# A four-block transformer stack on one core: the router's work re-ordered around the shared expert

## The chip, the core and the metric

The kernel runs on one core of one Trainium2 chip. Five engines work side by side, each through its own list of instructions in order: TensorE (PE in the profile), VectorE (DVE), ScalarE (ACT), GpSimd (POOL) and SyncE (SP, which only starts transfers here). They meet only through semaphores. The metric is the time of one execution on the device in microseconds (us); lower is better.

## The reference

`x` holds 8 blocks of 128 rows with 256 columns, `ctx` the same. Four layers follow each other, each on the layer norm of `x` and added to it:

```python
x = x + L0_xattn(layernorm(x), ctx)      # 16 heads over 256 positions, rotary, batch of 8
x = x + L0_ffn(layernorm(x))             # mixture of experts: 2 of 16, and a shared expert
x = x + L1_xattn(layernorm(x), ctx)      # 32 heads of 8, q and k RMS-normalised
x = x + L1_ffn(layernorm(x))             # dense + low-rank experts, 2 of 16
```

The change is in the second layer. With `t` one of the 1024 rows of the normalised input:

```python
scores = sigmoid(t @ router.T)                       # 16 numbers per row
pick the 2 best of 4 groups by (scores + e_bias), then the 2 best experts in them
weights = scores[picked] / (sum + 1e-20)
routed = sum over picked e: weight_e * relu(t @ up_e)**2 @ down_e
shared = relu(t @ shared_up)**2 @ shared_down        # 512 inner columns
```

The layer norm is `(x - mean) / sqrt(var + 1e-5)`. The RMS norm of the third layer is `v * rsqrt(mean(v*v) + 1e-6)` over 8 numbers.

## The kernel before, in words

**Stages.** A: the first attention, a loop over the 8 blocks (`NB`), in each 8 steps (`PAIRS`); at a step PE makes scores (L662), ACT takes the exponential (L1112), PE multiplies by the values (`pv`, L677). B: the router and the shared expert, then the routed experts. C: the second attention in 8 slots of 4 steps. D: the last layer. Each engine's order is written out by hand, in Python loops over numbered half-steps ("spots"); nothing is scheduled by a tool.

**End of stage A.** For block 7 the normalisation of finished blocks is put into the attention's gaps on DVE: at spot 2 `norm_stats(0, 6)` (means, variances and reciprocal roots of blocks 0 to 5) and two `normalize_ffn`, which write the normalised rows to `ffn_x(b)`; at spot 6 `flip_back(6)`, a transpose that gives `o3`; at spot 9 the rest for blocks up to 6. PE's output product of block 6 (L685, at spot 9) waits for `flip_back(6)`. After the loop `flip(7)`, a division on POOL and `flip_back(7)` follow.

**Stage B on PE** is the list `B_USES`: the 7 turns of rows on TensorE (`xT`, L754), the output product of block 7 (`wm`), then pieces of the shared expert and of the router between each other. The shared expert has 8 pieces `n` (2 halves of the rows, 4 groups of 128 inner columns); `up` is L766, `activate` on ACT is a relu and a square (L1181, L1183), `down` is L775. The logits are made transposed for 512 rows at a time (`lgT`, L823), copied by DVE, and turned back by PE (`lg`, L833). DVE copies every turned block from PSUM to `xnT` (L1647), which `up` and the logits read. ACT's exponential (L1189) starts the choice of experts on DVE (L1659 to L1681), which ends in `hot16`. `rank` on PE (L802 to L807) counts with `hot16` how many rows stand ahead, and DVE makes `slots` of it (L1685 to L1698).

**After `slots`.** POOL sends the 1024 rows to the two experts' places with 16 indirect transfers (`sorted_x`, L1414); then SP loads them back in tiles of 256 rows, and a loop over 16 tile pairs turns (L912), multiplies (L924), activates and multiplies again (L936). Beside the scatter, PE, ACT and DVE prepare the keys of stage C: `project_keys` (L953), squares on ACT (L1196), sums and a reciprocal root over 128x256 (L1771, `rsqrt`), scaling (L1775), the weights of the experts (L1709 to L1716) and `rest_keys(0)` (L1782). All this stands ahead of the first tile in DVE's list.

**`rsqrt`** (L1445) is a bit-trick guess and three Newton steps; each instruction waits for the one before by a semaphore (`Steps`). It is used by every `norm_stats`, once for the keys and once for each of the 8 blocks of stage C.

PSUM has 8 banks; `misc(u)` gives a use its bank in turn, and two semaphores, `misc_full` and `misc_free`, count the uses.

## Time and profile before

| | us |
|---|---|
| median of 3 runs (lowest, highest) | 421.08 (418.58, 422.0) |
| the profiled execution | 418.32 |
| its span, first to last instruction | 416.6 |
| PE busy | 301.3 (72%) |
| DVE busy | 302.5 (73%) |
| ACT busy | 162.3 (39%) |
| POOL busy | 99.5 (24%) |

So 1.7 us of the profiled execution lie outside its span, and it is 2.8 us under the median. The mean granted TensorE clock is 0.865 of full speed (full is 2.4 GHz, the other level 1.2 GHz). In the strip of 40 slices of 10.4 us each, the router and the shared expert take slices 16 to 20:

```profile
PE   4257788878867666999926999133787897587795
PEld 3222444434433323366815998011454554353453
DVE  6977888988988687364483655186689888776894
ACT  1103557656655650233322776001544445160101
POOL 1234445535522201000771111464000000000000
PEclk9755999999999988999975999755788869695999
```

Each digit is the busy share of a slice in tenths. No engine is busy all the time, and which one is waited for changes from stage to stage; so the time is read from the chain of work that ended last, and from each engine's list where that chain passes.

### The profile page before, as it was taken

The page shows a single profiled execution, that of the slowest core. Times are in us where ns is not written, and L with a number is a line of the kernel's source. Part 1 is how long each engine was busy: PE and PEld are TensorE (multiplying, and loading weights), DVE is VectorE, ACT ScalarE, POOL GpSimd, SP SyncE. Part 2 cuts the span into 40 slices and gives each one's busy share as a digit, 9 for nine tenths or more (in the row PEclk, how much of TensorE's full clock was granted, in tenths as well). Part 3 has the DMA queues.
Part 4 walks back from the last instruction along what each step waited for, and adds up shares of the span by engine and source line. Part 5 has one row for each costly group of instructions (what it writes and reads, how often), then busy time and mean ns, then how long its engine had stood idle before and what let it go on. Part 6 is the DMA issues. An engine that isn't in the chain of part 4 may idle for free.

```text
span 416.6 us, 7271 instructions
## 1 busy us (share of the span) xinstructions
PE 301.3 (72%) x2634; PEld 184.9 (44%) x2634; DVE 302.5 (73%) x826; ACT 162.3 (39%) x252; POOL 99.5 (24%) x194
## 2 busy tenths in 40 slices
PE   4257788878867666999926999133787897587795
PEld 3222444434433323366815998011454554353453
DVE  6977888988988687364483655186689888776894
ACT  1103557656655650233322776001544445160101
POOL 1234445535522201000771111464000000000000
PEclk9755999999999988999975999755788869695999
DMA  7593466876787340000225666734365555400011
GB/s 238 154 264 108 119 211 170 235 242 148 223 251 220 121 162 0 0 2 0 99 98 183 203 212 198 222 101 133 119 192 179 179 176 179 140 2 1 2 50 50
DMA packets 76387, 58.19 MB, mean 140 GB/s; under 512 B 5056, under 2 KB 73152, under 8 KB 76352
## 3 DMA queue, kind: packets, MB, share of 16 engines
q1 hardware_dynamic: 66688, 42.68, 34.2%
q10 hardware_dynamic: 8128, 10.85, 8.2%
q0 software_dynamic: 1536, 4.20, 3.2%
q8 instruction: 21, 0.34, 0.3%
q14 instruction: 14, 0.11, 0.1%
HBM read 32.87 MB, written 24.64 MB: 138 GB/s over the span
## 4 chain that ended last, share of the span: by engine, by line
DVE 36%; PE 36%; issue 9%; DMA 8%; POOL 7%; ACT 1%; SPq 1%; POOLq 0%; DVEq 0%
DVE mx L1498 8%; PE psum L924 4%; POOL sorted_x L1414 4%; PE psum L936 3%; PE psum L766 3%; PE psum L626 3%; PE psum L775 2%; PE psum L677 2%; PE psum L754 2%; PE psum L912 2%; DVE stats L1465 2%; PE psum L641 2%; DVE pvT L1811 2%; DVE rope_ab L1487 2%; DVE rs_a L1454 2%
## 5 line engine op out<-in xcount | busy, mean ns | idle before, releaser
L1498 DVE TENSOR_REDUCE mx<-psum 128x2 f32<-128x512 f32 x128 | 81.0, 682 | 13.6 <-PE psum L641 12.5
L1112 ACT ACTIVATE prob<-psum 128x1024 f32<-128x1024 f32 x64 | 64.0, 1022 | 43.4 <-PE psum L662 43.3
L641 PE MATMUL psum<-kstk,qstk 64*128 64x256 bf16 x256 | 27.3, 295 | 21.4 <-DVE mx L1498 12.1
L1282 ACT ACTIVATE prob<-psum 128x1024 f32<-128x1024 f32 x32 | 32.6, 1024 | 23.1 <-PE psum L884 22.9
L677 PE MATMUL psum<-prob,vt 128*32 128x256 f32 x512 | 35.8, 391 | 5.8 <-ACT prob L1112 4.7
L444 POOL TENSOR_TENSOR parts<-qk_rest,parts 128x256 bf16<-128x256 f32 (+1 forms) x15 | 13.5, 902 | 68.4 <-ACT parts L1257 64.9
L662 PE MATMUL psum<-qstk,kstk 64*128 64x256 bf16 x256 | 25.2, 281 | 0.8 <-DMA qstk<-mT 0.8
L641 PEld LDWEIGHTS psum<-kstk,qstk 64*128 64x128 bf16 x256 | 9.8, 98 | 34.8 <-DVE mx L1498 23.9
L900 PE MATMUL psum<-prob,vt 128*32 128x128 f32 x512 | 23.9, 314 | 0.2 <-ACT prob L1282 0.2
L677 PEld LDWEIGHTS psum<-prob,vt 128*32 128x32 f32 x512 | 16.2, 110 | 14.2 <-ACT prob L1112 6.0
L754 PE MATMUL psum<-eye,xn 128*128 128x128 f32 x32 | 8.5, 355 | 19.3 <-DVE xn L1763 11.3
L1055 PE MATMUL psum<-wd,xnT 128*128 128x512 f32 x32 | 17.0, 682 | 2.8 <-DVE xall L1807 2.8
L1418 POOL DMA_INDIRECT wup<-sorted_y,slots x16 | 15.3, 955 | 15.5 <-DMA sorted_y<-qstk 11.0
L662 PEld LDWEIGHTS psum<-qstk,kstk 64*128 64x128 bf16 x256 | 8.5, 95 | 21.5 <-issue 12.5
L924 PE MATMUL psum<-xnT,qstk 128*128 128x128 f32 x124 | 17.8, 289 | 0.1
L863 PE MATMUL psum<-wc,xT 128*128 128x256 f32 x32 | 14.2, 591 | 4.8 <-DVE qk_rest L1801 4.2
L900 PEld LDWEIGHTS psum<-prob,vt 128*32 128x32 f32 x512 | 14.0, 122 | 7.4 <-issue 4.9
L1414 POOL DMA_INDIRECT sorted_x<-qstk,slots x8 | 7.9, 993 | 37.7 <-DVE slots L1698 35.5
L924 PEld LDWEIGHTS psum<-xnT,qstk 128*128 128x128 f32 x124 | 16.3, 203 | 0.9 <-issue 0.5
L1119 ACT CAST parts<-qk 128x512 bf16<-128x512 f32 x8 | 4.9, 618 | 29.5 <-POOL qk L438 17.1
L936 PE MATMUL psum<-wdn,act 128*128 x62 | 16.1, 381 | 0.0
L1181 ACT ACTIVATE rel<-psum 128x512 f32<-128x512 f32 x8 | 4.8, 597 | 28.8 <-PE psum L766 28.8
(238 smaller groups left out, 634.3 us busy)
## 6 DMA issues: line engine op xcount, KB each, us to landing
qstk<-stack_scratch SPq DMA_DIRECT2D x32, 256.0 KB, 3.9
kstk<-stack_scratch SPq DMA_DIRECT2D x30, 256.0 KB, 3.5
stack_scratch<-parts SPq DMA_DIRECT2D x23, 192.0 KB, 2.2
prob<-sorted_x SPq DMA_DIRECT2D x15, 256.0 KB, 3.1
stack_scratch<-parts SPq DMA_DIRECT2D x25, 128.0 KB, 2.2
sorted_x<-zero_row ACTq DMA_DIRECT2D x3, 1024.0 KB, 4.9
wup<-in_wup ACTq DMA_DIRECT2D x4, 640.0 KB, 4.7
wdn<-in_wdn ACTq DMA_DIRECT2D x4, 640.0 KB, 6.1
```

The lines of the kernel that those rows point to most:

```text
L641: last = nc.tensor.matmul(banks[s][:, nb * D:(nb + 1) * D], qstk[par][rows, pair, nb * P:(nb + 1) * P], kstk[par][rows, pair, :], start=Tr ...
L662: last = nc.tensor.matmul(exp_buf(k)[:, s, mb * D:(mb + 1) * D], kstk[b % SETS][rows, k, mb * P:(mb + 1) * P], qstk[b % SETS][rows, k, :], ...
L677: last = nc.tensor.matmul(pv_bank(1)[32 * j:32 * j + 32, g * D:(g + 1) * D], vt[b % 2][:, mb, 4 * t + j, 8:40] if low else vt[b % 2][:, mb ...
L754: last = nc.tensor.transpose(bank[:, n * P:(n + 1) * P], blk, eye[:])
L900: last = nc.tensor.matmul(pv_bank(k // 2)[32 * j:32 * j + 32, g * P:(g + 1) * P], v[:, 8 * k + h, 8:40], prob[k % 2][:, at * P:(at + 1) * ...
L924: last = nc.tensor.matmul(psum[:, n % 2, t_ * P:(t_ + 1) * P], tile_w(n, t_)[:, f * P:(f + 1) * P], tile_xT(n)[:, (2 * t_ + f) * P:(2 * t_ ...
L936: last = nc.tensor.matmul(psum[:, 2 + n % 2, t_ * D:(t_ + 1) * D], act2[n % 2][:, t_ * P:(t_ + 1) * P], w, start=True, stop=True)
L1055: last = nc.tensor.matmul(psum[:, b % 4, :], xnT[:, f, b * P:(b + 1) * P], wd[:, f, :], start=(f == 0), stop=(f == 1))
L1112: nc.scalar.activation(prob[(b * PAIRS + k) % 3][:], exp_buf(k).rearrange("p a n -> p (a n)"), ACT.Exp, scale=SCALE).then_inc(exp_done, 1)
L1282: nc.scalar.activation(prob[k % 2][:], exp_buf(k).rearrange("p a n -> p (a n)"), ACT.Exp, scale=SCALE).then_inc(exp_done, 1)
L1414: nc.gpsimd.indirect_dma_start(sorted_x, row_of(k, b), ffn_x(b), None).then_inc(scattered, 16)
L1498: nc.vector.tensor_reduce(mx[:, half, :, 4 * s + p4:4 * s + p4 + 1], bank.rearrange("n (b m) -> n b m", b=2), AX_X, ALU.max).then_inc(misc ...
```

## The change

1. **Roots.** `rsqrt` makes its first guess in two instructions instead of three (a multiplication by -0.5 takes the place of the shift and the -1.0), and takes two steps of four instructions (a third-order step, with its constants folded into gains) instead of three steps of three. Ten instructions in place of twelve, wherever it is called.
2. **Rows only centred.** `ffn_x(b)` holds `x - mean`; the root is not needed for it. The logits are multiplied by `rstd`, the shared expert's result and the experts' weights by `inv_var = rstd * rstd` (relu squared of a scaled row is its square times that). `add_shared` becomes `scalar_tensor_tensor` with that scalar.
3. **DVE at block 7.** Only `bn_stats` of blocks 0 to 3 stands ahead of `flip_back(6)`; means and centring follow it, and one `roots_ffn(0, 7)` stands behind all centring, ahead of `flip(7)`.
4. **Turned rows** are copied to `xnT` by ACT (`take_x`) instead of DVE; PE turns blocks 0 and 1 within the attention of block 7 (spots 12 and 14).
5. **Logits** are made per block, with the rows as the stationary operand (`logits`, 4 instructions a block, 16 columns each), in one bank; `lgT`, its copies and its turning back are gone.
6. **PE's order**: all turns, logits 0 to 3, the output product of block 7, logits 4 to 6, one `up`, the turn and logits of block 7, another `up`, four pairs of `down` and `up`, then `rank`, then the rest of the shared expert. New semaphores replace `misc_full` and `misc_free` there.

The core of the diff (moved but unchanged lines are left out):

```diff
@@ PE
+            def turn_x(b):
+                pe.wait_ge(xn_ready, NB + b + 1)
+                if b < 2:
+                    pe.wait_ge(misc_free, A_END)
+                else:
+                    pe.wait_ge(xt_free, b - 1)
+                for f in range(2):
+                    last = nc.tensor.transpose(xt_bank(b)[:, f * P:(f + 1) * P], ffn_x(b)[:, f * P:(f + 1) * P], eye[:])
+                last.then_inc(xt_full, 1)
...
+                    if b == NB - 1 and spot in (12, 14):
+                        turn_x(spot // 2 - 6)
...
+            def logits(b):
+
+                pe.wait_ge(xt_free, b + 1)
+                if b == 0:
+                    pe.wait_ge(pv_free, NB + 2)
+                for f in range(2):
+                    last = nc.tensor.matmul(lg_bank[:, b * NE:(b + 1) * NE], xnT[:, f, b * P:(b + 1) * P], wr[:, f, :],
+                                            start=(f == 0), stop=(f == 1))
+                last.then_inc(lg_full, 1)
...
+            for b in range(2, NB - 1):
+                turn_x(b)
+            for b in range(4):
+                logits(b)
+            pe.wait_ge(o3_ready, NB)
+            output(wm_bank).then_inc(wm_full, 1)
+            for b in range(4, NB - 1):
+                logits(b)
+            up(0, 0)
+            turn_x(NB - 1)
+            logits(NB - 1)
+            up(0, 1)
+            for n in range(4):
+                down(n // N_SHARED, n % N_SHARED)
+                up((n + 2) // N_SHARED, (n + 2) % N_SHARED)
+            rank()
+            for n in range(4, 2 * N_SHARED):
+                down(n // N_SHARED, n % N_SHARED)
+                if n + 2 < 2 * N_SHARED:
+                    up((n + 2) // N_SHARED, (n + 2) % N_SHARED)
@@ ACT
+            def take_x(b):
+                act.wait_ge(xt_full, b + 1)
+                nc.scalar.copy(xnT[:, :, b * P:(b + 1) * P], xt_bank(b)[:, 0:D].rearrange("p (f n) -> p f n", f=2)
+                               ).then_inc(xt_free, 1)
+
+            for b in range(NB):
+                take_x(b)
+            activate(0, 0)
+            act.wait_ge(lg_taken, 1)
+            nc.scalar.activation(sc[:], sc[:], ACT.Exp, scale=-1.0).then_inc(sig_ready, 1)
+            for n in range(1, 2 * N_SHARED):
+                activate(n // N_SHARED, n % N_SHARED)
@@ DVE
-                for _ in range(3):
+                for gain in (1.0, STEP_GAIN):
                     steps.then(nc.vector.tensor_tensor(a, o, v, ALU.mult))
-                    steps.then(nc.vector.scalar_tensor_tensor(out=a, in0=a, scalar=-0.5, in1=o,
-                                                              op0=ALU.mult, op1=ALU.mult))
-                    steps.then(nc.vector.scalar_tensor_tensor(out=o, in0=a, scalar=1.5, in1=o,
+                    steps.then(nc.vector.tensor_tensor(a, a, o, ALU.mult))
+                    steps.then(nc.vector.scalar_tensor_tensor(out=a, in0=a, scalar=-10 / 3 * gain, in1=a,
+                                                              op0=ALU.add, op1=ALU.mult))
+                    steps.then(nc.vector.scalar_tensor_tensor(out=o, in0=a, scalar=5.0 * gain ** 2, in1=o,
                                                               op0=ALU.add, op1=ALU.mult))
...
                     if spot == 2 and b == NB - 1:
-                        norm_stats(0, B_EARLY)
+                        bn_stats_of(0, 4)
+                    if spot == 6 and b == NB - 1:
+                        steps.then(bn_stats_of(4, B_EARLY - 4))
+                        means(0, B_EARLY)
...
-                        norm_stats(B_EARLY, 1)
-                        normalize_ffn(B_EARLY)
+                        steps.then(bn_stats_of(B_EARLY, 1))
+                        means(B_EARLY, 1)
+                        for early in range(2, NB - 1):
+                            center_ffn(early)
+                        roots_ffn(0, NB - 1)
...
+            dve.wait_ge(lg_full, NB)
+            nc.vector.tensor_tensor(sc[:], lg_bank.rearrange("p (b e) -> p b e", e=NE), spread(rstd[:], NB, NE), ALU.mult
+                                    ).then_inc(lg_taken, 1)
+            nc.vector.tensor_tensor(inv_var[:], rstd[:], rstd[:], ALU.mult)
```

The three places where instructions move are shown as lists, in program order. First DVE around the transpose `o<-o` of block 6 (`flip_back(6)`; `rs_v`, `rs_a`, `rstd` are the root's numbers, `qstk` and `kstk` hold `ffn_x`). Before:

```order
L1465 BN_STATS stats<-xall 128x6 x6
L1472 BN_AGGR mv<-stats 128x2 x6
L1448 TENSOR_SCALAR rs_v<-mv 128x6
L1449 TENSOR_SCALAR rs_a<-rs_v 128x6
L1451 TENSOR_SCALAR rstd<-rs_a 128x6
...
L1481 TENSOR_SCALAR qstk<-xall,mv,rstd 128x256 x2
L1521 STREAM_TRANSPOSE o<-o 128x256
L1506 SCALAR_TENSOR_TENSOR xall<-psum,cb,xall 128x256
```

and DVE at the same place after the change:

```order
L1487 BN_STATS stats<-xall 128x6 x4
L1550 STREAM_TRANSPOSE o<-o 128x256
L1487 BN_STATS stats<-xall 128x6 x2
L1504 BN_AGGR mv<-stats 128x2 x6
L1508 TENSOR_SCALAR qstk<-xall,mv 128x256 x2
L1535 SCALAR_TENSOR_TENSOR xall<-psum,cb,xall 128x256
L1487 BN_STATS stats<-xall 128x6
L1504 BN_AGGR mv<-stats 128x2
L1508 TENSOR_SCALAR qstk<-xall,mv 128x256 x2
L1508 TENSOR_SCALAR kstk<-xall,mv 128x256 x3
L1469 TENSOR_SCALAR rs_v<-mv 128x7
```

Two statistics, six means, twelve instructions of roots and two normalisations stood ahead of the transpose and now stand behind it; the roots come once, behind the centring.

Second, PE from the last two products with the values (`psum<-prob,vt`) to `rank` (`psum<-hot,before`). Before, up to the second half's logits (L766 is `up`, L775 `down`, L754 a turn):

```order
L677 MATMUL psum<-prob,vt 32x256 x8
L754 MATMUL psum<-eye,qstk 128x128 x8
L754 MATMUL psum<-eye,kstk 128x128 x6
L685 MATMUL psum<-o,wa 128x256
L766 MATMUL psum<-xnT,wup 128x512 x4
L775 MATMUL psum<-wdn,act 128x256 x4
L823 MATMUL psum<-xnT,wr 16x512 x2
L754 MATMUL psum<-eye,kstk 128x128 x2
L823 MATMUL psum<-xnT,wr 16x512 x2
```

and PE after the change (L791 is `up`, L802 `down`, L705 a turn, L815 the logits):

```order
L705 MATMUL psum<-eye,qstk 128x128 x4
L690 MATMUL psum<-prob,vt 32x256 x8
L705 MATMUL psum<-eye,qstk 128x128 x4
L705 MATMUL psum<-eye,kstk 128x128 x6
L815 MATMUL psum<-wr,xnT 128x16 x8
L709 MATMUL psum<-o,wa 128x256
L815 MATMUL psum<-wr,xnT 128x16 x6
L791 MATMUL psum<-xnT,wup 128x512 x2
L705 MATMUL psum<-eye,kstk 128x128 x2
L815 MATMUL psum<-wr,xnT 128x16 x2
L791 MATMUL psum<-xnT,wup 128x512 x2
L802 MATMUL psum<-wdn,act 128x256 x4
```

Behind these, seven `up` and six `down` stood ahead of `rank` in all; now six `up` and four `down` do, and four `down` and two `up` follow it (before two and one).

## Rows read from the trace of the kernel before

**Rows 1.** The chain that ended last, in order of time: start, us, what
```profile
190.55 1.72 PE psum L766 x4
192.26 1.73 PE psum L775 x8
...
194.26 0.21 PE psum L807 x8
...
196.38 0.19 DVE slots L1698
...
219.49 2.90 DMA prob<-sorted_x
...
224.47 2.01 PE psum L924 x8
```

**Rows 2.** Timeline of PE: start, us, engine, line, names, count [idle before <-releaser]
```profile
139.25 0.60 PE L685 MATMUL psum<-o,wa 128*128 128x256 f32 x2
...
152.46 1.19 PE L685 MATMUL psum<-o,wa 128*128 128x256 f32 x2 [1.98 <-DVE o L1521]
...
157.46 1.07 PE L677 MATMUL psum<-prob,vt 128*32 128x256 f32 x16 [1.12 <-ACT prob L1112]
...
162.52 1.79 PE L754 MATMUL psum<-eye,kstk 128*128 128x128 f32 x6 [0.19 <-DVE xnT L1647]
...
172.65 0.44 PE L754 MATMUL psum<-eye,kstk 128*128 128x128 f32 x2
...
216.31 1.12 PE L964 MATMUL psum<-eye,qkn 128*128 128x128 f32 x4 [7.34 <-DVE qkn L1775]
...
372.40 1.07 PE L851 MATMUL psum<-w,eh 128*128 128x16 f32 x8 [0.96 <-DVE eh L1874]
```

**Rows 3.** Timeline of DVE, end of stage A and choice of experts
```profile
146.24 1.99 DVE L1465 BATCH_NORM_STATS2 stats<-xall 128x6 f32<-128x256 f32 x6
...
151.22 0.73 DVE L1481 TENSOR_SCALAR qstk<-xall,mv,rstd 128x256 f32<-128x256 f32 x2
...
158.69 0.71 DVE L1512 STREAM_TRANSPOSE pvT<-psum 128x512 f32<-128x512 f32 x1
...
160.67 0.45 DVE L1521 STREAM_TRANSPOSE o<-o 128x256 f32<-128x256 f32 x1 [0.88 <-POOL o L1365]
...
180.44 0.23 DVE L1659 TENSOR_SCALAR sc<-sc 128x128 f32<-128x128 f32 x1 [3.94 <-ACT sc L1189]
...
189.53 0.29 DVE L1681 TENSOR_TENSOR hot<-hot_all 128x128 bf16<-128x128 f32 x1
194.50 0.17 DVE L1685 TENSOR_SCALAR pages<-psum 128x16 int32<-128x16 f32 x1 [4.68 <-PE psum L807]
```

**Rows 4.** Timeline of ACT: a copy, and two exponentials of block 7
```profile
139.88 0.37 ACT L1130 COPY vt<-psum 128x256 f32<-128x256 f32 x1 [0.27 <-PE psum L685]
...
154.23 1.02 ACT L1112 ACTIVATE prob<-psum 128x1024 f32<-128x1024 f32 x1 [2.69 <-PE psum L662]
```

**Rows 5.** Windows of 2 us: PE, PEld, DVE, ACT, POOL busy, PEclk, DMA, GB/s
```profile
166.00:168.00 2.00, 2.00 (x6) 0.95 (x5) 1.69 (x10) 0.51 (x1) 0.00 (x0) 0.98 0.00 0
```

**Rows 6.** Timeline of DVE beside the scatter, the keys and the first tile
```profile
210.69 0.29 DVE L1449 TENSOR_SCALAR qk<-qk 128x256 int32<-128x256 int32 x1
...
219.71 0.69 DVE L1782 TENSOR_TENSOR qk_rest<-psum,kstk 128x512 f32<-128x512 f32 x1
223.65 0.69 DVE L1733 COPY xnT<-psum 128x512 f32<-128x512 f32 x1 [3.25 <-PE psum L912]
```

**Rows 7.** Timeline of DVE in stage C: a root over 128x32, first and last
```profile
306.69 0.24 DVE L1448 TENSOR_SCALAR rs_v<-ss,eps_v 128x32 f32<-128x32 f32 x1
...
309.42 0.42 DVE L1793 TENSOR_TENSOR qkn<-psum,rs 128x256 f32<-128x256 f32 x1
```

**Rows 8.** Timeline of POOL: two of the 16 scatters, the second beside DVE's wide root
```profile
202.75 0.96 POOL L1414 DMA_INDIRECT sorted_x<-qstk,slots  x1 [0.30 <-issue]
...
212.98 1.08 POOL L1414 DMA_INDIRECT sorted_x<-kstk,slots  x1 [0.30 <-issue]
```

254 lines of the change are left out of this document (107 added, 147 removed).

## The prediction

> **What bounds the kernel now.** I read the chain that ended last first. Between the end of the first attention and the first routed tile it runs: PE's pieces of the shared expert, `rank`, DVE to `slots`, 16 scatters on POOL, the load of the tiles, PE's tile loop [rows 1]. The reader is to see that ahead of `rank` stand an `up` of 1.72 us and a `down` of 1.73, and that no wait for DVE is named there. DVE's timeline says why: `hot16` was done at 189.53 + 0.29 = 189.82, and DVE then idled 4.68 us until `rank`'s result [rows 3]. So the router's result lay ready for over 4 us while PE worked through its list; what stands in PE's list ahead of `rank` is the bound, not the choice of experts. `rank` ended at 194.47 and `slots` at 196.57 [rows 1].
>
> Next, the end of the attention in PE's timeline: the output product of block 6 at 152.46 had waited 1.98 us for DVE's transpose, and ran 1.19 us instead of the 0.60 of its like at 139.25; the last product with the values ran from 157.46 to 158.53 [rows 2]. ACT's exponential at 154.23 had idled 2.69 us behind it [rows 4]. DVE made its roots and normalisations ahead of that transpose [rows 3].
>
> Last, what lies in the shadow of the scatter. From `slots` (196.57) to the tile loads' end (219.49 + 2.90 = 222.39) is 25.8 us [rows 1]. DVE meanwhile finished the keys at 219.71 + 0.69 = 220.40 and waited 3.25 us before the first tile's copy at 223.65 [rows 6]. That is the slack which anything made later on PE, ACT or DVE after `rank` can use.
>
> **The change, part by part** (clock times are those of the profiled execution).
>
> *End of the attention.* After the change the transpose of block 6 stands behind four statistics of 0.33 us (1.99 for six, from 146.24 [rows 3]), so it ends at about 148.0, before PE asks for it at 152.46 - 1.98 = 150.48 [rows 2]. The output product then runs 150.5 to 151.1 at 0.60; scores, the two exponentials of 1.02 [rows 4] and the products of 1.07 [rows 2] follow in turn: scores to 151.4, the exponential behind its predecessor 151.5 to 152.5, products to 152.6, scores to 153.0, the last exponential to 154.0, the last products 154.05 to 155.1. Gain 158.5 - 155.1 = **3.4 us**. If the clock falls all the same, the product costs 1.19 instead of 0.60, and with the others slow as well I count back 1.5 us: bounds 1.9 and 3.4. I take 3.4, because the idle time ahead of the slow spell is what is removed.
> DVE's moved work stays off PE's way: from 151.1 a sum, a statistic and a mean (about 1.1), five centrings at 0.33 (0.73 for two [rows 3], the second's tail overlapping), ten root instructions at about 0.225 (below) end at 156.1; then flip, reciprocal, POOL's division and the transpose back, 160.67 + 0.45 - 158.69 = 2.4 us from the flip's start [rows 3], so `o3` is there at 158.5. PE wants it at 159.8 (next sum).
>
> *PE's list from there to `rank`.* Before: 158.53 to 194.47, 35.9 us. After, if PE never waits:
> - 5 turns; ACT copies instead of DVE (0.37 against about 0.4 [rows 4]), two banks in turn; six rows (three turns) took 1.79 us [rows 2]: 5 x 0.55 = 2.75, bounds 2.2 and 3.0;
> - 32 logit instructions; nearest is L851, same shape 128x16, eight in 1.07 with the last one's tail: 32 x 0.125 = 4.0;
> - output product 0.60;
> - 6 `up` x 1.72 = 10.3 and 4 `down` x 1.73 = 6.9 [rows 1];
> - the eighth turn 0.44 [rows 2], its copy 0.37 and the handing over: 0.95; `rank` 0.5.
>
> Sum 26.0, so `rank` ends at 155.1 + 26.0 = 181.1, **9.9 us** gained beside the 3.4. Does PE wait? The eighth turn needs block 7 centred: output product at 160.4, sum, statistic, mean, centring on DVE 1.6 us more: 162.0; PE is in `up` until 163.6. `hot16`: the last logits end at 165.0, DVE scales them (0.3), ACT's exponential stands behind `activate(0, 0)` and ends at 166.1, and from there the choice takes 189.82 - 180.44 = 9.4 us [rows 3]: 175.5. PE reaches `rank` at 180.6, so 5 us of slack there. The same 2.1 us lead to `slots` at 183.2, against 196.57: **13.3 us** earlier.
>
> *After `rank`.* Now four `down` and two `up` (10.3 us) follow where two and one stood (5.2): relative to `rank`, PE's keys come 5.2 us later. DVE gets back 0.8 us in the wide root (one instruction like the shift, 0.29 alone and 0.33 in step [rows 6], one of about 0.46) and pays 0.2 for the multiplication by `inv_var`. `add_shared` in its new form costs at most 0.15 us more for each of 8, hidden, since DVE waits for the keys' squares behind it. So DVE is free for the first tile at 220.4 - 13.3 + 5.2 - 0.6 = 211.7, while the tile path would want it at 223.65 - 13.3 = 210.3: **1.3 us lost**. Against that stands TensorE's clock. Before, PE idled 7.34 us ahead of turning the keys at 216.31 [rows 2] and again until the tiles; the first tile's eight products took 2.01 us [rows 1], at 1.2 GHz, where eight at 2.4 GHz are about 0.9. After, keys and tiles follow each other without a gap, from 207.4 on, and PE, steadily at work from 162.52, had a granted clock of 0.98 (2.4 GHz nearly throughout) from 166 on [rows 2, 5]. If so, the first products and turns gain up to 1.7 us. I take the two together as +0.4 gained; bounds -1.3 and +1.7.
>
> *Roots elsewhere.* A root over 128x32 took 309.42 - 306.69 = 2.73 us for 12 instructions, 0.227 each [rows 7]; two less save 0.45. On the chain lie: the first layer norm ahead of the first loads, seven of the eight roots of stage C (the third one, of block 2, runs while PE waits for a transfer), the two of stage D. 10 x 0.43 = **4.3 us**; bounds 2 (stage C partly waits for PE) and 5.
>
> **Sum.** 3.4 + 9.9 + 0.4 + 4.3 = 18.0 us off 418.32 gives 400.3. The median of the runs was 2.8 us above the profiled execution; on its scale the sum is 403.1. I forecast between them: **402 us**. Its own range, from the bounds (1.5 and 1.7 and 2.3 us less gained, not all at once; 1.3 and 0.7 more): 397 to 406.
>
> **Rivals.**
> *The keys become the bound (0.18).* For it: 5.2 us of delay against 3.25 of slack, and ACT, PE and DVE hand over to each other there four times, with PE at half clock if it idles. If PE's clock is down for the six remaining pieces and the keys as well, or down in the turns and logits (where PE hands every block to ACT), 4 to 7 us of the gain go: 406 to 410. Against: pieces of the shared expert follow without gap.
> *The gain is larger (0.07).* PE wins back clock through the denser stages: below 397.
> *It does not do what it says (0.04).* `slots` come earlier but the tile loop starts as before, since something in the shadow (the keys) takes it all: only the roots and the attention's end remain, or the roots alone: 414 to 421.
> *Slower (0.03).* One mechanism: POOL's scatters. Each takes 0.96 us; those beside DVE's wide root took 1.08, so DVE's work cost them 0.12 [rows 8]. PE and DVE now have more work beside them. The gain is eaten at 18.0 / 16 = 1.1 us more for each, that is when one takes 2.1 us; at 2.4 us (1.44 more, 16 times, 23 us) the end is 425. Against: nearly the same DVE instructions ran beside them before, and nothing stretched by more than 0.12.
> The Trainium skill (SBUF — State Buffer, "SBUF: two separate sides") says that GpSimd cannot write the descriptors of its own transfers while VectorE runs in a two-port mode; the page counts float32 copies within SBUF among the causes, and `tensor_tensor` and `tensor_reduce` not. By that rule the new work should hold up no scatter, since the root is now nearly all of two-operand forms; the 0.12 us were lost beside such forms too, which the rule does not give. Neither changes the sum.
>
> **How the numbers follow.** The forecast (397 to 406) gets 0.68, the rivals 0.18, 0.07, 0.04 and 0.03. Half the keys' case and the larger gain are taken in: 396 to 409 holds over 8 in 10. A measurement of this kernel can tell about 1% from no change. Faster by over 1% are the first three cases: 0.93; within 1%: 0.04; slower: 0.03.
>
> **What would show it.** Right: no idle time on PE ahead of the output product of block 6; last products with the values at about 155; `rank` near 180.6, no wait named for DVE's `hot16`, DVE idle some 5 us ahead of it; `slots` near 183; first tile's copy at 211 to 212 with hardly an idle time ahead; 10 instructions a root. Wrong: PE idle between turns and ACT's copies of more than 0.2 us each; logits of more than 0.15 us an instruction; a granted clock of 0.5 between 155 and 165 or at the first tile; POOL's transfers above 1.1 us; stage C as long as before.

## The result

The changed kernel took 408.71 us (median of 4 runs, 407.19 to 410.48) where the kernel before took 421.54 (4 runs, 418.58 to 422.55): a ratio of 0.971, with a 95% interval of 0.964 to 0.978. Forecast were 402.0 us, with 397 to 406 as its own range and 396 to 409 as the wider one: the sign was right, and the time lies outside the first range and at the very end of the second. Run again unaltered on other chips, the same kernel took 409.74, 422.51 and 419.95 us, with before at 421.48, 420.99 and 419.82 beside it. So there are two things to explain: 6.7 us that were missing at once, and 10 us more that are lost on some chips. Ratios and intervals, here and below, leave out disturbed executions, over 1.5% above the fastest of their kernel, so a ratio need not be the quotient of two medians (of "old root" below two of four executions are left, of "flip behind" two of eight). The profiled execution took 407.19 us, with a span of 405.4 against 416.6 before.

The page of the changed kernel, first part and granted clock (columns as on the page of before):

```profile
span 405.4 us, 7267 instructions
PE 300.0 (74%) x2650; PEld 187.4 (46%) x2650; DVE 290.6 (72%) x777; ACT 164.4 (41%) x260; POOL 98.9 (24%) x194
PEclk9755799999999998899979999555998989777997
```

PE's timeline from the last block's attention to the last logits (start, us, engine, line, names, count, idle before):

```profile
150.69 0.70 PE L709 MATMUL psum<-o,wa 128*128 128x256 f32 x2
...
154.39 1.07 PE L690 MATMUL psum<-prob,vt 128*32 128x256 f32 x16 [0.53 <-ACT prob L1129]
...
157.59 2.14 PE L815 MATMUL psum<-wr,xnT 128*128 128x16 f32 x16
159.57 1.20 PE L709 MATMUL psum<-o,wa 128*128 128x256 f32 x2
160.56 2.58 PE L815 MATMUL psum<-wr,xnT 128*128 128x16 f32 x12
162.98 3.37 PE L791 MATMUL psum<-xnT,wup 128*128 128x512 f32 x4
```

Two things are to be seen against [rows 2]. The output product of block 6 at 150.69 waits for nothing, and the last products with the values end at 154.39 + 1.07 = 155.46 instead of 158.53. But from 159.57 on every piece takes nearly twice what it should: the output product 1.20, the twelve logits 2.58 (0.215 each), an `up` 3.37. The windows of 2 us (PE, PEld, DVE, ACT, POOL busy, PEclk, DMA, GB/s) say why:

```profile
158.00:160.00 2.00, 2.00 (x14) 2.00 (x15) 0.37 (x1) 0.16 (x1) 0.98 (x3) 0.75 0.00 0
160.00:162.00 2.00, 2.00 (x10) 1.82 (x9) 1.04 (x3) 0.00 (x0) 0.00 (x0) 0.50 0.03 8
162.00:164.00 2.00, 2.00 (x8) 1.48 (x8) 1.69 (x11) 0.00 (x0) 0.00 (x0) 0.50 0.00 0
164.00:166.00 2.00, 2.00 (x4) 0.87 (x3) 0.20 (x2) 0.00 (x0) 0.00 (x0) 0.54 0.00 0
166.00:168.00 2.00, 1.54 (x8) 0.89 (x7) 0.24 (x2) 1.36 (x3) 0.00 (x0) 1.00 0.00 0
```

PE is busy in all of it but the last window, and yet has 1.2 GHz (0.50) for six microseconds. DVE's timeline at the rank and at the first tile:

```profile
183.75 0.17 DVE L1713 TENSOR_SCALAR pages<-psum 128x16 int32<-128x16 f32 x1 [5.94 <-PE psum L828]
...
185.63 0.17 DVE L1726 CAST slots<-slot_f 128x16 int32<-128x16 f32 x1
...
213.50 0.69 DVE L1813 TENSOR_TENSOR qk_rest<-psum,kstk 128x512 f32<-128x512 f32 x1
214.11 1.28 DVE L1763 COPY xnT<-psum 128x512 f32<-128x512 f32 x2
```

The rank came at 183.7, and DVE had waited 5.94 us for it, so PE's list is still what bounds the slots. At the first tile DVE had no idle time left: where it waited 3.25 us before [rows 6], the keys now bound it.

Stage by stage, all in us and all from the two profiled executions:

| stretch | before | after | gain | forecast |
|---|---|---|---|---|
| start to the last block's maxima in TensorE's hands | 143.99 | 144.27 | -0.3 | +0.4 |
| to the last product with the values | 14.54 | 11.19 | 3.35 | 3.4 |
| to the rank's end | 35.9 | 28.25 | 7.7 | 9.9 |
| rank to the end of the tile loop | 66.5 | 66.4 | 0.1 | 0.4 |
| tile loop to the first expert sum | 9.8 | 9.15 | 0.65 | 0 |
| stage C, to the last norm's statistics | 82.7 | 81.8 | 0.9 | 3.0 |
| stage D and the end | 63.1 | 64.3 | -1.2 | +0.9 |

This table is one profile against one, and some of its rows don't repeat. The changed kernel was profiled four times in all, and the kernel before twice:

| stretch | before | before again | changed | again | third | fourth |
|---|---|---|---|---|---|---|
| last block's maxima to the last product with the values | 14.5 | 14.5 | 11.2 | 14.4 | 14.4 | 14.5 |
| from there to the rank's end | 35.9 | 36.0 | 28.25 | 31.3 | 31.3 | 28.3 |
| stage C | 82.7 | 83.6 | 81.8 | 83.9 | 82.9 | 82.4 |
| stage D and the end | 63.1 | 62.2 | 64.3 | 63.1 | 60.5 | 64.3 |

So the 3.35 us at the end of the attention were there in one profile of four, and the slots, at 185.6 us in the first, came at 190.5 to 191.0 in the other three. PE's timeline of the third profile there, and two windows, show why (columns as above):

```profile
149.64 1.93 PE L690 MATMUL psum<-prob,vt 128*32 128x256 f32 x16 [0.69 <-ACT prob L1129]
...
152.04 1.22 PE L709 MATMUL psum<-o,wa 128*128 128x256 f32 x2
```
```profile
144.00:146.00 2.00, 1.36 (x12) 0.44 (x8) 1.49 (x4) 1.03 (x2) 0.34 (x1) 0.50 0.31 65
...
150.00:152.00 2.00, 2.00 (x20) 0.53 (x12) 0.00 (x0) 0.50 (x1) 0.00 (x0) 0.50 0.26 62
```

The output product of block 6 waits for nothing here either, but PE has 1.2 GHz from 144 to 154 and makes each set of products with the values in 1.93 us instead of 1.07. Of the 16 profiles of the changed kernel and its variants, 11 have this spell and 14.4 to 14.5 us in the stretch, and 5 have 11.2. What decides between the two stays open.

In stage C the chain of the first profile after the change runs through SyncE and its transfers, where that of the first profile before hardly did. The chain that ended last, part of block 3 (start, us, what):

```profile
282.31 3.80 DMA stack_scratch<-parts
286.12 0.36 SPq L589
...
288.10 3.39 DMA stack_scratch<-wa
...
291.55 2.27 DMA kstk<-stack_scratch
```

and the wait that goes with it (engine, line, waited for: us in total, times, longest):

```profile
PE psum L901 <- DMA qstk<-stack_scratch: 7.0, 4, 2.6
```

### The profile page after: what moved, and what is told of

It reads as the page before. It is cut to its first block, busy times and chain, and to the rows that moved or that the text cites. A ratio compares the mean times of both kernels' runs of the same rounds, so it can differ in the third digit from the quotient of the medians.

```text
span 405.4 us, 7267 instructions
## 1 busy us (share of the span) xinstructions
PE 300.0 (74%) x2650; PEld 187.4 (46%) x2650; DVE 290.6 (72%) x777; ACT 164.4 (41%) x260; POOL 98.9 (24%) x194
## 4 chain that ended last, share of the span: by engine, by line
PE 41%; DVE 30%; DMA 12%; issue 6%; POOL 4%; SPq 4%; ACT 3%; DVEq 0%; POOLq 0%
DVE mx L1527 8%; PE psum L791 4%; DMA stack_scratch<-parts 4%; PE psum L941 4%; PE psum L690 4%; PE psum L802 3%; PE psum L953 3%; PE psum L639 3%; PE psum L654 2%; PE psum L1088 2%; DVE rope_ab L1516 2%; PE psum L970 2%; PE psum L780 2%; DMA stack_scratch<-wa 2%; DMA kstk<-stack_scratch 2%
## 5 line engine op out<-in xcount | busy, mean ns | idle before, releaser
L1527 DVE TENSOR_REDUCE mx<-psum 128x2 f32<-128x512 f32 x128 | 81.1, 682 | 15.7 <-PE psum L654 14.4
L1303 ACT ACTIVATE prob<-psum 128x1024 f32<-128x1024 f32 x32 | 32.5, 1023 | 26.9 <-PE psum L901 26.7
L690 PE MATMUL psum<-prob,vt 128*32 128x256 f32 x512 | 35.9, 392 | 5.3 <-ACT prob L1129 4.2
L917 PE MATMUL psum<-prob,vt 128*32 128x128 f32 x512 | 22.6, 301 | 0.2 <-ACT prob L1303 0.2
L901 PE MATMUL psum<-qstk,kstk 64*128 64x128 bf16 x256 | 13.9, 236 | 7.3 <-DMA qstk<-stack_scratch 7.0
L675 PEld LDWEIGHTS psum<-qstk,kstk 64*128 64x128 bf16 x256 | 8.5, 95 | 20.7 <-issue 13.3
L941 PE MATMUL psum<-xnT,qstk 128*128 128x128 f32 x124 | 16.8, 278 | 1.3 <-DVE xnT L1763 1.2
L917 PEld LDWEIGHTS psum<-prob,vt 128*32 128x32 f32 x512 | 13.3, 117 | 7.3 <-issue 4.3
L791 PE MATMUL psum<-xnT,wup 128*128 128x512 f32 x32 | 16.6, 646 | 0.0
L941 PEld LDWEIGHTS psum<-xnT,qstk 128*128 128x128 f32 x124 | 15.2, 192 | 2.3 <-DVE xnT L1763 1.6
```

Source lines behind the costliest of these rows:

```text
L675: last = nc.tensor.matmul(exp_buf(k)[:, s, mb * D:(mb + 1) * D], kstk[b % SETS][rows, k, mb * P:(mb + 1) * P], qstk[b % SETS][rows, k, :], ...
L690: last = nc.tensor.matmul(pv_bank(1)[32 * j:32 * j + 32, g * D:(g + 1) * D], vt[b % 2][:, mb, 4 * t + j, 8:40] if low else vt[b % 2][:, mb ...
L791: last = nc.tensor.matmul(psum[:, n % 2, :], wup[:, f, NE + g, :], xnT[:, f, c * HALF:(c + 1) * HALF], start=(f == 0), stop=(f == 1))
L917: last = nc.tensor.matmul(pv_bank(k // 2)[32 * j:32 * j + 32, g * P:(g + 1) * P], v[:, 8 * k + h, 8:40], prob[k % 2][:, at * P:(at + 1) * ...
L941: last = nc.tensor.matmul(psum[:, n % 2, t_ * P:(t_ + 1) * P], tile_w(n, t_)[:, f * P:(f + 1) * P], tile_xT(n)[:, (2 * t_ + f) * P:(2 * t_ ...
L1303: nc.scalar.activation(prob[k % 2][:], exp_buf(k).rearrange("p a n -> p (a n)"), ACT.Exp, scale=SCALE).then_inc(exp_done, 1)
```

## The experiments

Eighteen runs followed, in sets that each shared a chip and the runs of before; a ratio is to those of before in the same set. The last four columns are from the profiled execution: "attention's end" is the last block's maxima to the last product with the values, "values to slots" goes from there to the slots, "slots to tile" to the first tile's copy, and "stage C" is the first expert sum to the last norm's statistics.

| kernel | median, us | ratio (95%) | attention's end | values to slots | slots to tile | stage C |
|---|---|---|---|---|---|---|
| before | 421.5 | | 14.5 | 37.9 | 27.3 | 82.7 |
| changed | 408.7 | 0.971 (0.964 to 0.978) | 11.2 | 30.2 | 28.5 | 81.8 |
| set 1: changed, old root | 413.8 | | 14.5 | 30.2 | 29.2 | 84.1 |
| before, new root | 420.2 | 1.000 (0.996 to 1.003) | 14.4 | 39.6 | 27.0 | 82.3 |
| changed, queries first | 404.1 | 0.960 (0.957 to 0.964) | 14.5 | 30.2 | 28.5 | 77.7 |
| before, queries first | 420.2 | 0.999 (0.996 to 1.002) | 14.5 | 37.9 | 27.1 | 82.7 |
| set 2: weights late | 420.4 | 0.999 (0.995 to 1.003) | 14.4 | 33.2 | 37.6 | 82.3 |
| logits behind | 419.8 | 1.001 (0.998 to 1.004) | 14.5 | 26.9 | 38.8 | 81.8 |
| flip behind | 423.5 | 0.990 (0.983 to 0.997) | 14.5 | 30.2 | 38.9 | 82.9 |
| rank early | 420.4 | 1.000 (0.996 to 1.003) | 11.2 | 26.8 | 40.8 | 81.9 |
| set 3: changed again | 422.5 | 1.002 (0.996 to 1.008) | 14.4 | 33.2 | 38.9 | 83.9 |
| before again | 421.2 | 0.998 (0.990 to 1.007) | 14.5 | 37.9 | 28.7 | 83.6 |
| queries first, weights late | 417.2 | 0.985 (0.977 to 0.994) | 11.2 | 30.1 | 37.7 | 80.7 |
| turns twice | 418.4 | 0.989 (0.981 to 0.997) | 11.2 | 27.7 | 39.4 | 82.3 |
| set 4: changed, third time | 409.7 | 0.974 (0.966 to 0.981) | 14.4 | 33.2 | 28.5 | 82.9 |
| VectorE copies | 414.6 | 0.977 (0.968 to 0.986) | 11.2 | 30.2 | 31.1 | 84.2 |
| scatters behind | 428.8 | one run | 14.5 | 30.2 | 45.3 | 83.6 |
| VectorE copies, queries first | 409.6 | 0.970 (0.963 to 0.977) | 14.4 | 30.2 | 31.1 | 79.6 |
| set 5: changed, fourth time | 420.0 | 2 runs | 14.5 | 30.2 | 38.8 | 82.4 |
| VectorE copies, queries first | 418.9 | 0.997 (0.994 to 1.000) | 14.5 | 30.2 | 39.9 | 78.1 |

### Where the roots' gain went: SyncE's list

The roots were to give 3.0 us in stage C and gave 0.9. Two kernels change the root alone, in either kernel:

```
...
-                for gain in (1.0, STEP_GAIN):
+                for _ in range(3):
...
-                    steps.then(nc.vector.tensor_tensor(a, a, o, ALU.mult))
-                    steps.then(nc.vector.scalar_tensor_tensor(out=a, in0=a, scalar=-10 / 3 * gain, in1=a,
-                                                              op0=ALU.add, op1=ALU.mult))
+                    steps.then(nc.vector.scalar_tensor_tensor(out=a, in0=a, scalar=-0.5, in1=o,
+                                                              op0=ALU.mult, op1=ALU.mult))
...
```

(this is the changed kernel with the old root, whose first guess in three instructions comes back too; the other kernel has the same edit the other way round, in the kernel before)

> The changed kernel with the root of before (12 instructions). Prediction on record: the ten-step root is worth about 4.3 us outside the router, so this kernel would be 4 to 5 us slower than the changed one. Theory now (SyncE's list of transfers sets the pace of the second attention, so that shorter roots only make VectorE wait longer): the stretch from the first expert sum (259.3 us in the changed kernel) to the statistics of the last norm (341.2), 81.9 us there, stays within 1.2 us, and the whole is at most 2.5 us slower, of which the wide root of the keys is 0.8.

> The kernel before with the ten-step root alone. Prediction on record: 4.3 us and more faster (416.5 on the median's scale). Theory now: the stretch of the second attention was 82.8 us before and was close to SyncE's pace already, so it gains at most 1.5 us; all in all 1 to 2.5 us faster than before.

and two exchange a pair of transfers in SyncE's list of stage C, again in either kernel:

```
                 keys_c_to_dram(b)
+                queries_c_to_dram(b)
                 sp.wait_ge(st_full, NB * PAIRS + (b - 2) * C_STEPS + 4)
                 keys_c_from_dram(b)
-                queries_c_to_dram(b)
                 queries_c_from_dram(b)
```

> The changed kernel, and in the second attention SyncE writes the queries of a block ahead of loading its keys, so that it no longer stands still for the 3 us in which the keys' write lands. If SyncE's list sets the pace, the stretch of 81.9 us falls by 2 to 4 us and TensorE no longer waits for the query loads (7.0 us there in the changed kernel); if VectorE does, it stays within 0.7.

> The kernel before with the same exchange in SyncE's list. If SyncE's pace bound only the changed kernel (whose roots are shorter), the stretch of 82.8 us stays within 0.7 here; if it bound both, it falls by 1 to 2 us. Rival: the transfers themselves take longer when queries and keys are written together, and it grows.

Measured: the new root in before gives nothing (ratio 1.000; 1 to 2.5 us had been expected), and neither does the exchange in before (0.999). The old root in the changed kernel has 84.1 us in stage C, more than the 1.2 us above 81.8 that were expected; but the changed kernel itself had up to 83.9 in its four profiles, so this run alone doesn't show what the old root costs there. The exchange in the changed kernel takes stage C to 77.7 and the whole to 404.1 us, and PE's waits at L901 for `qstk<-stack_scratch` are gone from its waits. That chip had no run of the changed kernel, but sets 3 to 5 have one each: beside it on the same chip, kernels with the exchange have 80.7 against 83.9, 79.6 against 82.9 and 78.1 against 82.4.

PE's scores, which waited for no transfer in the first profile of before, do wait with the new root in it, and do in the second profile of before itself too (in this order; columns as above):

```profile
PE psum L886 <- DMA qstk<-stack_scratch: 6.3, 4, 2.1
```
```profile
PE psum L884 <- DMA qstk<-stack_scratch: 4.5, 3, 2.3
```

What follows: stage C has two limits close to each other, DVE's work for a block, and SyncE's list, where the queries' write stands behind the keys' load, which stands behind the landing of the keys' write. With the old root or the old order of transfers the stage takes 82 to 84 us, whichever of the two it is, and so close that either can come last from one profile to the next. Either edit alone is hidden by the other limit; with both it takes 77.7 us, 5 less than the kernel before with the exchange alone on the same chip, and 78.1 to 80.7 in the other sets.

### TensorE's clock ahead of the rank

PE's list took 28.25 us instead of 26.0, with PE at 1.2 GHz for about 7 us while it was busy. Three kernels move or add work there. In "logits behind" PE takes the output product, the first `up`, the last turn, and then all logits together; in "turns twice" the turns of blocks 2 to 7 run twice, into the same bank, to fill PE's idle time of the attention (the result stays the same); in "flip behind" DVE's order at block 7 is that of before, with the centrings and the root ahead of the flip. The first two edits:

```
-            for b in range(4):
-                logits(b)
             pe.wait_ge(o3_ready, NB)
             output(wm_bank).then_inc(wm_full, 1)
-            for b in range(4, NB - 1):
-                logits(b)
             up(0, 0)
             turn_x(NB - 1)
-            logits(NB - 1)
+            for b in range(NB):
+                logits(b)
             up(0, 1)
```
```
-                for f in range(2):
+                for f in (0, 1, 0, 1) if b >= 2 else (0, 1):
```

> The changed kernel with the output product of block 7 and one up ahead of all logits, which then stand in one piece behind the eighth turn. In the changed kernel the granted clock fell to 0.5 at 158.5 and came back at 166. If the logits' small products (16 columns) let the clock fall, the output product and the up run at 2.4 GHz and a fall comes later or not at all; if the spell was set by what came before 158 (turns with idle time between), it falls at the same place and costs the same 3.6 us. From the last product with the values (155.5) to rank's end (183.7) are 28.2 us in the changed kernel; 25 without a slow spell.

> The changed kernel with each turn of the blocks 2 to 7 done twice (16 us of TensorE's otherwise idle waits filled at most; no result is changed). Theory that TensorE's idle time ahead of 158 us costs the granted clock behind it: with more work there the clock falls less or later, and the stretch from the last value product to the rank (28.2 us) shrinks by up to 3.6 us, less the 0.35 us that the last block's second turn adds. Rival, that the fall comes from the work that is there anyway (full busyness): it stays 28.2 us or longer, with the same level of 0.5 in it.

> The changed kernel with VectorE's order at block 7 as before: statistics, means and roots of six blocks and two centrings ahead of the transpose of block 6. By the prediction TensorE waits again, about 1.5 to 2 us, at the output product of block 6, and the last product with the values ends 1.5 to 3.4 us later against the start of block 7. Rival: TensorE's gap was only moved, and the distance stays within 0.5.

PE's timeline of "logits behind" from the output product on:

```profile
162.76 0.70 PE L709 MATMUL psum<-o,wa 128*128 128x256 f32 x2 [0.33 <-DVE o L1547]
163.30 1.88 PE L791 MATMUL psum<-xnT,wup 128*128 128x512 f32 x4
...
165.46 3.64 PE L815 MATMUL psum<-wr,xnT 128*128 128x16 f32 x32
```

and the window in which only logits run (columns as above):

```profile
167.00:169.00 2.00, 2.00 (x20) 2.00 (x19) 0.00 (x0) 0.19 (x1) 0.00 (x0) 1.00 0.00 0
```

Here the 32 logits take 3.64 us. This profile has the earlier spell, 0.50 from 147 to 155, but from the last product with the values on the clock stays at 2.4 GHz, and PE's list from the last product with the values (160.14) to the rank (184.82 + 0.35) takes 25.0 us. So the forecast's sum for this list (26.0) was right for a full clock, even a little high, and the clock is what was missing: 28.25 - 25.0 = 3.2 us. "Turns twice" keeps the clock at 1.00 as well and takes 2.5 us off the stretch to the slots, though it does more work. The two differ in what they keep. "Turns twice" keeps the order, with 16 logits ahead of the output product, and fills the waits for ACT's copies; "logits behind" keeps those waits and puts an `up` ahead of the narrow products. Neither the waits alone nor the early logits alone made the clock fall in these profiles, both together did, in all 14 profiles of kernels that have both. Each of the two exceptions rests on one profile. How long the spell lasts isn't fixed: until 166 in the first profile, until 174 in the third of the same kernel, with 33.2 us to the slots instead of 30.2.

"Flip behind" puts roots and centrings ahead of the transpose of block 6 again, which the output product of that block waits for; what they cost is to be read in the attention's end. It took 14.5 us, and PE waited for no transpose: the transpose ended at 152.46, and PE, at 1.2 GHz by then, asked for it at 153.28 only. The changed kernel itself has 14.4 to 14.5 us whenever that spell comes. So in the spell this edit of the change is worth nothing; at full clock, where PE asked at 150.69, it wasn't measured. The stretch behind, to the slots, stays at 30.2 us.

### The keys, now the bound of the first tile

```
-            expert_weights()
             rest_keys(0)
...
                 if n in (4, 8, 11):
                     rest_keys(n // 4 + n // 11)
+                if n == 6:
+                    expert_weights()
```

> The changed kernel with the experts' weights (7 VectorE instructions, 1.9 us) moved from ahead of the first tile to behind the sixth. If VectorE's work on the keys is what the first tile now waits for, the time from slots (185.8) to the first copy of a tile (214.1), 28.3 us, falls by 1.3 to 1.9 us, down to the 26 to 27 us that scatter and load take. If the scatter and the load are the bound, it stays within 0.4.

In "rank early" one pair of `down` and `up` is moved from ahead of the rank to behind it:

```
-            for n in range(4):
+            for n in range(3):
...
-            for n in range(4, 2 * N_SHARED):
+            for n in range(3, 2 * N_SHARED):
```

> The changed kernel with rank one pair of down and up (3.45 us) earlier; the choice is ready by then (VectorE idled from 177.7 to 183.7). If TensorE's whole list and the keys behind it are the bound, slots come 3.4 us earlier and the first tile's copy and everything behind it do not move (within 0.5). If slots are the bound, the first tile's copy comes 2.5 to 3.4 us earlier.

Both fell on a chip where the whole stretch was longer (next part), and are compared with their neighbours there. Taking the weights' seven instructions from ahead of the first tile shortens the stretch by 1.2 us (37.6 against 38.8, and 37.7 against 38.9 in set 3), a little under the 1.3 to 1.9 that were expected. An earlier rank moves the slots 3.4 us forward and lengthens the stretch behind them by 2.0, so that the copy comes 1.4 us earlier, where at most 0.5 or at least 2.5 was expected; with late signals in that stretch it decides nothing. So the work on the keys bounds the first tile after the change, as forecast, by the first run and by the missing idle time in the first profile.

### The same kernel at 422 us: signals that come late beside the scatters

Sets 2, 3 and 5 gave medians of 417.2 to 423.5 us for everything built on the changed kernel. Is it the variants or the chip? The controls, unaltered:

> The changed kernel itself, unaltered. Four variants of it (the owner's weights later, the logits together behind, the flip behind, the rank earlier) took 420 to 423 us where the kernel before took 420; in all four profiles 10 us are lost at one place, between the slots and the first tile's copy (37.6 to 40.8 us, against 28.5 in the changed kernel's profile): ScalarE stands up to 5.8 us ahead of its copies of the context and its squares, while the scatters run. Two of the variants change only VectorE's order and cannot touch ScalarE's list. If the stall belongs to the chip or the hour and not to the variants, this kernel shows it in some runs too, and its time is near 420 when it does and 408 to 410 when it doesn't; if it belongs to the variants, this kernel stays at 407 to 411 with 28.5 us at that place.

> The kernel before, unaltered, for its profile on this chip. Its time stayed within 418 to 423 us on both chips, so a stall of ScalarE beside the scatters should be absent from it: slots to first copy 27.3 us, as in its first profile. If it has the stall as well, other stretches are shorter than in the first profile.

> The changed kernel with SyncE's queries ahead of its key loads (it gave 404.1 us alone) and the experts' weights computed at the seventh pair of tiles instead of ahead of the first. If the keys bound the first tile's copy, the second edit takes 1.3 to 1.9 us off the 28.5 us from the slots to that copy, and the whole comes to 402 to 403 us; if ScalarE's stall comes, 10 us are lost there instead and it comes to 412 to 415.

It is the chip, or the hour: the unaltered kernel took 422.5 us, and loses 10.4 us between the slots and the first tile. The kernel with queries first and the weights late took 417.2 us, more than the 412 to 415 that were expected with that loss. ACT's timeline there, in that control, and PE's:

```profile
204.18 0.60 ACT L1217 ACTIVATE sq<-psum 128x512 f32<-128x512 f32 x1 [2.97 <-PE psum L970]
207.02 0.59 ACT L1240 COPY ctx_all<-psum 128x512 f32<-128x512 f32 x1 [2.25 <-remote]
213.37 0.60 ACT L1217 ACTIVATE rel<-psum 128x512 f32<-128x512 f32 x1 [5.77 <-remote]
214.81 0.59 ACT L1240 COPY ctx_all<-psum 128x512 f32<-128x512 f32 x1 [0.84 <-remote]
```
```profile
202.53 0.60 PE L962 MATMUL psum<-eye,ctx_all 128*128 128x128 f32 x4
202.96 1.89 PE L970 MATMUL psum<-wc,ctx_all 128*128 128x256 f32 x8
...
207.75 2.60 PE L970 MATMUL psum<-wc,ctx_all 128*128 128x256 f32 x8 [2.46 <-issue]
```

The copy at 207.02 needs the turn that PE's row ends at 203.13; the square at 213.37 needs the product that ends at 204.85: it came 8.5 us late, with ACT idle for 5.77 of them. (The ends of PE's rows are modelled, so these profiles don't tell whether the result or only its signal was late; PE took ACT's signals within 0.2 us here.) In the first profile the four squares follow each other at 1.7 to 2.2 us with no such wait, though the scatters run beside them there too. "Remote" means that the profile knows no sender for what ended the wait. All of it lies beside the second half of POOL's 16 scatters, which themselves take their usual 0.96 us (POOL's timeline of the same run, the first, the ninth and the last):

```profile
192.04 1.20 POOL L1435 DMA_INDIRECT sorted_x<-qstk,slots  x1 [30.61 <-DVE slots L1726]
...
202.42 0.96 POOL L1435 DMA_INDIRECT sorted_x<-kstk,slots  x1 [0.30 <-issue]
...
211.27 0.96 POOL L1435 DMA_INDIRECT sorted_x<-kstk,slots  x1 [0.30 <-issue]
```

The kernel before meets it too, against what was expected, in its profile of the same set (ACT's timeline):

```profile
210.26 0.60 ACT L1196 ACTIVATE rel<-psum 128x512 f32<-128x512 f32 x1 [2.30 <-remote]
215.24 0.60 ACT L1196 ACTIVATE act<-psum 128x512 f32<-128x512 f32 x1 [4.38 <-remote]
```

These are 6.7 us of waits, but only 1.5 us more from the slots to the first tile. Before, the context's first copy came 3.8 us behind the slots, so that only the last two squares were left when the signals grew late, and the 3.25 us of slack at the first tile [rows 6] took most of that. The change brings the rank, and so the scatters, ahead of six pieces of the shared expert; the first copy now comes 9.0 us behind the slots, nearly the whole chain of copies and squares lies in the scatters' second half, and there is no slack behind it. "Rank early" goes one step further that way and has the longest stretch of all (40.8).

Is it ACT's own? The copies and squares go to VectorE (lines shortened):

```
-                nc.scalar.copy(ctx_all[...], psum[:, 4 + p % 2, :])
+                nc.vector.tensor_copy(ctx_all[...], psum[:, 4 + p % 2, :])
-                nc.scalar.activation(k_squares(p), psum[:, p, :], ACT.Square)
+                steps.then(nc.vector.tensor_copy(k_squares(p), psum[:, p, :]))
+                nc.vector.tensor_tensor(k_squares(p), k_squares(p), psum[:, p, :], ALU.mult)
```

and for the cause the scatters are held until the last square:

```
             pool.wait_ge(slots_ready, 1)
+            pool.wait_ge(k_squared, CTX_PAIRS)
```

> The changed kernel, unaltered, as the control of this set. It shows one of the two states seen so far: 407 to 411 us with 28.5 us from the slots to the first tile's copy, or 420 to 425 us with 38 to 40 us there and ScalarE standing about 9 us in all ahead of its copies and squares.

> The changed kernel with the copies of the turned context and the squares of the keys on VectorE instead of ScalarE (a square takes two instructions there, a copy and a product, so four times 0.6 us more). If the stall is ScalarE's own, the 38 to 40 us from the slots to the first tile's copy fall to 30 to 32 (28.5 plus the 2.4 us at most that VectorE's longer squares cost), and the time to about 411 to 414. If whatever engine does this work beside the scatters is held up, VectorE shows the same waits with its inputs ready and the stretch stays at 38 us or more. In the state without the stall this kernel is 1 to 3 us slower than the control.

> The changed kernel with GpSimd's 16 scatters held until the last square of the keys is done; only for what ScalarE does beside them. If the scatters hold ScalarE up, its copies and squares run as in the first profile (last square 17.8 us behind the slots), and the stall, if it lasts as long as the scatters, meets the next ScalarE instructions behind the gate. If they are not the cause, ScalarE stands 9 us as in the control, at the same place. The gathers of rows start some 17 us later than in the first profile in either case, so the time is 420 to 428 us and says nothing by itself.

> The kernel with VectorE's copies and squares, and SyncE's queries ahead of its key loads besides (alone it took 4.6 us off the changed kernel). In the state with the stall: 406 to 410 us, which would beat both kernels there by over 2%. In the state without it: 404 to 407, no better than the SyncE order alone (404.1).

This set fell on a chip that doesn't do it: the control took 409.7 us with 28.5 us in the stretch. So it says nothing on the cause; the run with the scatters held back shows no wait, but there was none to be taken away. It tells the price of VectorE's longer squares, 2.6 us (31.1 against 28.5). The last set:

> The changed kernel as the control once more: 407 to 411 us with 28.5 us from the slots to the first tile's copy, or 420 to 425 us with 38 to 40 us there.

> VectorE's copies and squares with SyncE's queries first, again. It took 409.6 us (31.1 us from the slots to the first tile's copy) on a chip without the stall. If the control shows the stall and it is ScalarE's own, this kernel keeps 31 us there and 406 to 412 us in all; if any engine is held up that does this work then, it shows 38 us or more there and 415 us or more.

Here the control has it (420.0 us, 38.8 in the stretch), and so has the kernel with VectorE's copies. DVE's timeline of that kernel, and PE's:

```profile
205.62 0.69 DVE L1849 COPY ctx_all<-psum 128x512 f32<-128x512 f32 x1 [4.18 <-remote]
...
213.37 0.69 DVE L1849 COPY ctx_all<-psum 128x512 f32<-128x512 f32 x1 [5.02 <-remote]
```
```profile
203.39 0.60 PE L962 MATMUL psum<-eye,ctx_all 128*128 128x128 f32 x4
```

The turn that ended at 203.99 reached DVE at 213.37. So it isn't ScalarE's own: the engine that takes PE's result waits, whichever it is, and moving the work from one to the other is no cure (39.9 us, and 418.9 in all). What holds the signal up stays open. It was seen only beside scatters, and in all nine profiles of the changed kernel and its variants that had it, the last late signal came 2.4 to 2.6 us after the end of the last scatter's row; that points at the scatters. But the one run that takes them away from that place was on a chip without it, so it isn't shown. Nor is it shown that the chip decides, and not the hour: the five sets ran on five chips, each once. And only one execution of each kernel was profiled; on the chips with late signals some others were as fast as 412.4 and 414.0 us, and what happened in them isn't known.

## Why the forecast was right, and where it was wrong

Two steps failed. The roots outside the router were put at 4.3 us on the chain and came to -0.6 in the three stretches where they lie, which is 4.9 of the 6.9 us missing between the two profiled executions. And TensorE's clock was taken as full from the end of the attention to the rank, which cost 2.2 there at once and, in the other profiles of the same kernel, most of the gain at the attention's end as well.

- **End of the attention, 3.4 us.** The first profile has 3.35, but by luck. The transpose of block 6 was ready and the output product ran without a wait, in all four profiles; but in three of them PE had 1.2 GHz all the same, and the gain was 0.1. The reason given for 3.4, that the idle time ahead of the slow spell is what is removed, is wrong: the spell comes without it. And the bound of 1.9 for that case is too high, since the spell was some 10 us long, where before it had been 3 to 4.
- **PE's list to the rank, 9.9 us.** The step that failed: it gave 7.7 in the first profile, and 4.6 in two others. Its sum was made at full clock throughout, and "logits behind" shows that it holds at full clock (25.0 us for 26.0). The changed kernel has 1.2 GHz from about 159 to 166, which cost 3.2 us against the 25.0. The forecast had named the sign of it (a granted clock of 0.5 between 155 and 165) among what would prove it wrong, and had a price for it in the keys' case, but put nothing of it in the sum, and PE was without idle time when the clock fell.
- **What hides the router.** Right: the choice of experts was ready 5.9 us ahead of the rank, as the forecast's 5. The lead on the slots was 196.57 - (185.63 + 0.17) = 10.8 instead of 13.3, which is mostly the clock again; in the other three profiles the slots stood at 190.7 to 191.2.
- **After the rank, +0.4.** Nearly right, by both of its terms: the keys bound the first tile (no idle time ahead of the copy), and the first tile's eight products took 1.16 us instead of 2.01. The sum came to +0.1.
- **Roots elsewhere, 4.3 us.** This step failed: -0.3 of 0.4 at the start, 0.9 of 3.0 in stage C, -1.2 of 0.9 in stage D. The root itself gave what was reckoned (ten instructions, 0.83 us less for the wide one). In stage C the step failed that counted seven roots on the chain because DVE was on it before: SyncE's list stood close behind it. The exchange in SyncE's list brings out the rest, and more. At the start the root's gain was there (the first row maxima begin at 22.20 instead of 23.23) and was gone by 144; PE's clock was 0.67 against 0.71 from 20 to 60. At the end the last products ran at 1.2 GHz (next row, PE's timeline of the changed kernel; before, the same four instructions took 1.13 us), which made the way from the last adapter's input to the end 2.8 us longer. The third profile of the same kernel has 2.4 GHz there and 60.5 us in stage D, so the program doesn't fix where such a spell falls; whether the change makes one likelier there isn't shown:

```profile
396.10 2.07 PE L1088 MATMUL psum<-wb,wxaT 128*128 128x256 f32 x4
```

- **The scale and the range.** The forecast stood 1.7 us above its own sum on the profiled scale (400.3), because the median of before was higher than its profile. The profile after was 1.5 us below its median too, so that was right. The lower end of its own range, 397, doesn't follow from its terms: 400.3 less 2.0 is 398.3.
- **The rival of the keys (0.18, 406 to 410)** gave the right time. Its mechanism, PE's clock down in the turns and logits, is what took 3.2 us; the keys' delay took no more than the 1.3 us that the forecast had in its sum, and the rest was lost in stages C and D, of which the rival said nothing.
- **The rival of the scatters (0.03, slower)** did not happen as it was told: a scatter took 0.96 or 0.97 us in the changed kernel (the first 1.21, as before), with no stretching at all, also beside `tensor_tensor` and reductions, which is what the Trainium skill's rule (SBUF — State Buffer, "SBUF: two separate sides") gives. Single scatters were stretched in two variants, to 1.11 us with the old root and to 1.18 where they were held back. But the place was right, as sets 2, 3 and 5 show: what is put beside the scatters can lose all that the change gains, by late signals and not by slower scatters.

## What to carry to other kernels

When work is made shorter on the chain, look for the second limit right behind it, an in-order transfer queue above all: here two edits that were each worth nothing on the kernel before took stage C down by 5 us together. Price a list of small products at half clock too, and put wide products ahead of the narrow ones; the same instructions took 28.2 us or more in one order and 25.0, in one profile, in another. Profile a kernel more than once before a stretch's gain is put down to an edit: 3.35 us at the attention's end were 0.1 in three other profiles. And measure on more than one chip before a gain is believed: the best version depends on it, with 404.1 us (0.960 of before) for the changed kernel with queries first where signals were prompt, and 417.2 us (0.985) for the same with the weights late where they weren't.

## What the runs showed of the hardware

- TensorE's granted clock fell to 1.2 GHz while the engine was fully busy, with turns, short waits and 16-column products ahead of the fall, and stayed there for some 7 us in one profile and 14 in another of the same kernel. Either filling the waits or a 512-column product ahead of the narrow ones kept it at 2.4 GHz, in one profile each.
- The same program met a slow spell in one execution and not in another: at the attention's end 1.2 GHz for some 10 us in 11 of 16 profiles, with no idle time of PE over 1.9 us ahead, and 2.4 GHz throughout in 5.
- On three of the chips a signal from TensorE reached ScalarE or VectorE up to 10 us after the row of the work had ended (the product that ended at 196.74 and the square at 206.70 in "turns twice"), in the second half of 16 scatters, with both kernels; in the profiles of the first result and of sets 1 and 4 never.
- A write to DRAM whose landing a queue waits for before its next transfer cost that queue 2.5 to 3.8 us each time on the changed kernel's chain ("DMA stack_scratch<-parts", "<-wa" and "<-qstk"), beside 2.3 to 3.2 us for the loads on it.
